# Two orders of VectorE passes, and a spread of reciprocals by float32r products, in a two-layer transformer kernel

## The reference

```python
def reference(x, f, ...):                      # x, f: (16, 256, 256)
    # layer 0
    q = x + embed[stage][:, :, None]
    c = softmax(q @ f^T) @ f                   # first attention, one head of 256
    x = x + attn0(c)                           # 16 heads of 16, causal, rotary q and k
    #   probs = softmax(scores / 4); out = probs @ v; out @ w_out^T + b_out
    c2 = x @ W_cat[cat] + b_cat[cat]
    x = x + fp4_ffn(c2)                        # 256 -> 704 -> 256, all operands quantised:
    #   scale = max|.| over 16 / 6; q = grid(x / scale) * sign * scale
    # layer 1
    y = zX * lap_x(x) + zY * lap_y(x) + zR * x * (1 - x)   # "field", neighbours with reflection
    x = x + attn1(rmsnorm(y) * g)              # 16 heads of 64, segments of 128, 16 memory rows
    x = x + moe(experts_of(x))                 # gelu, 16 experts by index, then top 2 of 8
    return x
```

## Time and profile before

| | |
|---|---|
| median of 3 runs | 2429.3 us (2426.37 to 2429.45) |
| the profiled execution, its own time | 2426.79 us |
| its span | 2424.7 us |
| busy share of the span: PE, PEld, DVE, ACT, POOL | 93%, 84%, 76%, 53%, 42% |
| chain that ended last, by engine | PE 58%, DVE 19%, POOL 8%, issue 7%, ACT 6%, DMA 1% |
| mean granted TensorE clock | 0.975 |
| layer 0 in the trace | up to about 790 us; one batch every 41.8 us |
| layer 1's attention | about 700 to 1500 us; one batch every 44.9 us |
| experts | from about 1500 us on |

### The profile page before, as it was taken

One profiled execution on the slowest core, in us unless ns is written; L12 is line 12 of the kernel. 1 busy time (PEld: TensorE's weight loads), 2 busy tenths in 40 slices (PEclk: granted clock), 3 DMA queues, 4 the chain that ended last, 5 costly groups with the idle time before them and its releaser, 6 DMA issues.

```text
span 2424.7 us, 53715 instructions
## 1 busy us (share of the span) xinstructions
PE 2248.6 (93%) x18240; PEld 2041.3 (84%) x18240; DVE 1852.2 (76%) x5119; ACT 1292.3 (53%) x3839; POOL 1019.9 (42%) x1078
## 2 busy tenths in 40 slices
PE   3799999999976899999999999899999999999999
PEld 2688878888865778888888887899999999999999
DVE  5878888888878666666666765578878888888876
ACT  1667666666662455655555554433336555555522
POOL 5535454454525455455555553033332222222073
PEclk8999999999997899999999999999999999999999
DMA  4523333333330322222222222222126777777443
GB/s 138 182 85 107 103 95 116 91 113 95 99 110 3 99 57 58 72 60 58 70 64 57 66 57 75 64 36 43 39 94 213 233 235 237 233 232 239 142 120 124
DMA packets 203301, 267.36 MB, mean 110 GB/s; under 512 B 61670, under 2 KB 171510, under 8 KB 192278
## 3 DMA queue, kind: packets, MB, share of 16 engines
q1 hardware_dynamic: 194166, 245.27, 33.4%
q0 software_dynamic: 8864, 18.66, 2.9%
HBM read 175.84 MB, written 43.94 MB: 91 GB/s over the span
## 4 chain that ended last, share of the span: by engine, by line
PE 58%; DVE 19%; POOL 8%; issue 7%; ACT 6%; DMA 1%; SPq 0%; POOLq 0%; DVEq 0%; ACTq 0%
PE bank L55 48%; PE bank L136 6%; POOL P L1796 2%; DVE xe L928 2%; PE bank L1322 2%; DVE Ph L821 2%; DVE tb L1654 1%; DVE qm L917 1%; DVE xe L933 1%; DVE sgs L955 1%; ACT P L1495 1%; PE bank L1362 1%; ACT Ph L657 1%; DVE rot0s L881 1%; DVE hb L965 1%
## 5 line engine op out<-in xcount | busy, mean ns | idle before, releaser
L1495 ACT ACTIVATE P<-P,mx 128x144 f32<-128x144 f32 x512 | 206.2, 405 | 229.2 <-DVE mx L1616 228.2
L2642 POOL DMA_INDIRECT xE<-d_y,ixs x78 | 112.1, 1437 | 336.2 <-PE bank L136 300.7
L55 PE MATMUL bank<-xD_hi,w1e_lo 128*128 128x256 f32 x880 | 251.1, 285 | 0.0
L55 PE MATMUL bank<-w2e_hi,hrD_hi 128*128 128x256 f32 x880 | 249.0, 283 | 0.0
L55 PE MATMUL bank<-w2e_lo,hrD_hi 128*128 128x256 f32 x880 | 248.9, 283 | 0.0
L55 PE MATMUL bank<-w2e_hi,hrD_lo 128*128 128x256 f32 x880 | 248.9, 283 | 0.0
L55 PE MATMUL bank<-xD_lo,w1e_hi 128*128 128x256 f32 x880 | 245.9, 279 | 0.0
L55 PE MATMUL bank<-xD_hi,w1e_hi 128*128 128x256 f32 x880 | 245.6, 279 | 0.0
L1127 POOL TENSOR_TENSOR xe<-xe 128x704 f32<-128x704 f32 (+3 forms) x64 | 88.0, 1375 | 353.9 <-DVE xe L936 353.7
L1796 POOL TENSOR_TENSOR P<-P,rs 128x512 f32<-128x512 f32 x128 | 133.1, 1040 | 246.0 <-DVE rs L1625 243.5
L2251 ACT ACTIVATE hD<-bank,b1E 128x256 f32<-128x256 f32 x312 | 127.0, 473 | 197.2 <-PE bank L55 182.8
(11 more groups left out here) (324 smaller groups left out, 7959.7 us busy)
## 6 DMA issues: line engine op xcount, KB each, us to landing
w1raw<-in_ew SPq DMA_DIRECT2D x39, 1024.0 KB, 5.9
w2raw<-in_ew SPq DMA_DIRECT2D x39, 1024.0 KB, 4.9
stack<-d_rot SPq DMA_DIRECT2D x256, 96.0 KB, 2.7
K<-Kn SPq DMA_DIRECT2D x256, 72.0 KB, 2.0
d_rot<-QKh SPq DMA_DIRECT2D x64, 256.0 KB, 3.1
Q<-Qn SPq DMA_DIRECT2D x256, 64.0 KB, 2.0
d_ys<-oE SPq DMA_DIRECT2D x39, 256.0 KB, 2.6
d_rot<-QKl SPq DMA_DIRECT2D x32, 256.0 KB, 3.1
```

The source lines that it names most:

```text
L55: inst = e.matmul(out, l, r, start=k == 0, stop=k == len(pairs) - 1)
L1495: inst = e.activation(P1[t % 2][:, n, :], P1[t % 2][:, n, :], ACT.Exp, bias=mx1[t % 2][:, 2 * g + sg:2 * g + sg + 1], scale=-1.0, accum_ou ...
L2642: e.indirect_dma_start(out=xE[q % 2][c], out_offset=None, in_=d_y, in_offset=bass.IndirectOffsetOnAxis(ap=ixs[r % 4][:, c:c + 1].bitcast(U ...
```

## The change

It has three parts. In layer 0, `invert_sums` makes the reciprocal, its high part rounded to float32r and the rest, side by side in a zeroed buffer `rsp` of 128 columns a half; it stands behind the first half's scales in slot 7. PE turns the 128 columns, ACT copies 128 rows as float32r, and `spread_sums` multiplies by `sel0r`, which has two ones a row of output (for the high and the low part), in float32r. In layer 0's order, the second half's scales move from slot 0 to the end of slot 7, ahead of the first half's last two steps; PE takes `values` and `turn_sums` ahead of `first_values`, and ACT `sums_copy` ahead of `x1_high`. In layer 1, `rotate(b + 1, 2)` and `rotate(b + 1, 3)` come earlier and the field's three passes later.

```diff
-        w_out0, rsT, OT0 = tile("w_out0", 2, 256), tile("rsT", 256), tile("OT0", 2, 256)
+        w_out0, rsT, OT0 = tile("w_out0", 2, 256), tile("rsT", 256, dt=F32R), tile("OT0", 2, 256)
-        tile("space_q", 552)
+        rsp, sel0r = tile("rsp", 2, 128, dt=F32R), tile("sel0r", 2, 128, dt=F32R)
+        tile("space_q", 40)
@@ turn_sums, spread_sums (PE)
-                turn(e, [(banks[6][0:16, st * 128:st * 128 + 128], rs0[b % 2][:, st, :]) for st in range(2)]
+                turn(e, [(banks[6][:, st * 128:st * 128 + 128], rsp[:, st, :].bitcast(F32)) for st in range(2)]
-                    inst = e.matmul(halves(7)[:, G, :], sel0[0:16, G, :], rsT[0:16, :], start=True, stop=True)
+                    inst = e.matmul(halves(7)[:, G, :], sel0r[:, G, :], rsT, start=True, stop=True)
@@ layer 0's loop (PE)
-                    if p == 0:
-                        first_values(b + 1)
-                        turn_sums(b - 1)
                     if p % 2 == 0:
                         values(P // 2 - 1)
+                    if p == 0:
+                        turn_sums(b - 1)
+                        first_values(b + 1)
@@ ACT
-                e.activation(rsT[0:16, :], banks[6][0:16, 0:256], ACT.Copy).then_inc(c_rsT, 1)
+                e.activation(rsT, banks[6][:, 0:256], ACT.Copy).then_inc(c_rsT, 1)
+                e.activation(sel0r, sel0, ACT.Copy)
                         first_copy(b + 1)
+                        sums_copy(b - 1)
                         x1_high(b + 1)
-                        sums_copy(b - 1)
@@ invert_sums (DVE)
                 e.wait_ge(c_P, 16 * (b + 1))
-                e.reciprocal(rs0[b % 2], rs0[b % 2]).then_inc(v_ri, 1)
+                if b:
+                    e.wait_ge(p_rsT, b)
+                else:
+                    e.wait_ge(g_V, 2)
+                inv, hi, lo = rs0[b % 2], rsp[:, :, 0:16], rsp[:, :, 16:32]
+                e.reciprocal(inv, inv).then_inc(*vs.up())
+                e.wait_ge(s_v, vs.n)
+                e.tensor_copy(hi, inv).then_inc(*vs.up())
+                e.wait_ge(s_v, vs.n)
+                e.tensor_tensor(lo, inv, hi.bitcast(F32), ALU.subtract).then_inc(v_ri, 1)
@@ layer 0's loop (DVE)
                     if p == 0:
-                        hidden_scales(b - 2, 1)
                         x1_low(b + 1)
                         hidden_steps(b - 2, 1)
                     if p == 7:
                         hidden_scales(b - 1, 0)
+                        invert_sums(b)
                         gated(b - 1, 1, 0)
                         gated(b - 1, 1, 1)
                         multiply(b - 1, 1, 0)
                         hidden_steps(b - 1, 0, (0,))
                         multiply(b - 1, 1, 1)
+                        hidden_scales(b - 1, 1)
                         hidden_steps(b - 1, 0, (1, 2))
-                        invert_sums(b)
@@ layer 1's loop (DVE), ahead of the maxima
                     if s == 2:
-                        rotate(b + 1, 2)
+                        rotate(b + 1, 3)
@@ behind the maxima
                     if s == 2:
-                        rotate(b + 1, 3)
+                        field(entering(b))
+                        field_sum(entering(b))
                     copy_turned(t)
+                    if s == 1:
+                        rotate(b + 1, 2)
-                    if s == 1:
-                        field(entering(b))
-                        field_sum(entering(b))
```

More of the change, by code:

```diff
@@ L313, in sync_ab @@
             load_in(0)
-            for dst, src in ((raw0, "w_qkv0"), (b_qk0, "b_qk0"), (rot0, "rot0k"), (sel0[0:16], "sel0"),
+            for dst, src in ((raw0, "w_qkv0"), (b_qk0, "b_qk0"), (rot0, "rot0k"), (sel0, "sel0"),
                              (w_out0, "w_out0"), (b_out0, "b_out0")):
@@ L1147, in pool_ab @@
             e.wait_ge(s_const, 1)
+            e.memset(rsp.bitcast(F32), 0.0)
             for i in range(2):
@@ L2744 @@
     A["w_out0"] = T2(np.ascontiguousarray(g["L0_attn_w_out"].T[rows]))
-    sel = np.zeros((16, 2, 128), np.float32)
+    sel = np.zeros((128, 2, 128), np.float32)
     for r in range(256):
-        sel[rows[r] // 16, r // 128, r % 128] = 1.0
+        sel[rows[r] // 16::16, r // 128, r % 128][0:2] = 1.0
     A["sel0"] = sel
```

## The result

The changed kernel takes 2437.29 us (median of 12 runs, 2432.41 to 2440.34). The kernel before took 2429.64 us (median of 12, 2425.57 to 2430.81) on the same chip. The ratio is 1.0033, with a 95% interval of 1.0025 to 1.0040, so the change makes the kernel slower by 7.7 us. The profiled execution took 2439.2 us, with a span of 2437.1 us, where before's had 2424.7. The spans differ by 12.4 us. 4.7 us of that is where each profiled execution happens to lie in its own runs.

The account below looks back on a forecast made before the run. VectorE was taken to set the time for 12 us of each layer 0 round, so PE savings there gain nothing. Terms 17.6 - 15.0 + 1.7 + 0.4 = +4.7 us gave 2434.0 us on the median, range 2412 to 2446.

Parts of the forecast that it names:

- The mechanism: Layer 0 loses as VectorE's steps take turns with POOL's delayed passes; layer 1 gains from an earlier rotation; chance 0.45.
- Layer 0's border: Layer 0, slot 7 to slot 1's maxima: those maxima come 1.26 us later a round, +17.6 us over 14 borders.
- rival B: Layer 0: holds don't add up, so it gains 0 to 0.5 us a round; 2413 us in all; chance 0.20.
- D: Layer 0: step 0 misses POOL's first pass or POOL keeps the port; +1.66 to +2.1 a round, 2440 to 2446; chance 0.18.
- E: PE's bound is elsewhere and both layers' new orders are absorbed; 2430 us; chance 0.05.
- list of signs: Expected changed profile, including steps 1 and 2 at 1.5 and 1.6 us, layer 0 rounds of 43.0, layer 1 of 43.7.
- I count them at nothing: Layer 0, PE: shorter spread (0.55 to 0.8 us) and removed PT wait (0.34 us) gain nothing, hidden behind VectorE.
- Layer 1: Earlier rotation 2 ends PE's wait for it; gain 1.15 us a round (0.9 to 1.35), -15.0 us over 13 rounds.
- Rival C: Layer 1 gives nothing, the field holding slot 2's copy by what the rotation frees; +19.7, 2449 us; chance 0.12.
- The join: Where the layers join: two more layer 0 borders cost +2.5, moving the field returns 0.8; +1.7, bounds -3 and +5.
- The start: Kernel start: one more ACT copy of 256 columns and one memset ahead of the first weights; +0.4 us.

Follow-up runs that it names:

- filled wait: Changed kernel plus three PE products per round, result overwritten, ahead of the wait for `hq` in slot 1; ratio 0.9980 to the kernel before.
- (a): Kernel before with layer 1's new order, and layer 0's three second-half steps moved behind the next slot's maxima; ratio 0.9910 to the kernel before.
- (b): Changed kernel with the second scales back in slot 0 and the second-half steps moved behind the next maxima; ratio 0.9929 to the kernel before.
- (c): Changed kernel, scales left in slot 7, with the second-half steps moved behind the next maxima; ratio 0.9953 to the kernel before.
- second set: The next four follow-up kernels after the first four, each run in turn with the kernel before on one chip; before's median there 2429.4 us.

## Why the prediction was right, and where it was not

The forecast was 2434.0 us with 2412 to 2446, "slower" the likeliest at 0.51. Measured were 2437.3 us and a ratio of 1.0033. The mechanism holds. The sum was +4.7 us. Measured were +7.7 on the medians and +12.4 between the traces. That the medians came so near is in part luck, as the sum at the end of this section shows.

**Layer 0's border** came out as it was laid down. The table shifts the changed trace by 29.87 us, so that the first scales' small pass stands where it stood before, 427.31:

| | forecast | measured |
|---|---|---|
| gate starts | 428.62 | 428.54 |
| step 2 of the first half ends | 433.87 | 433.87 |
| POOL starts | 434.10 | 434.01 |
| step 0 asked for | 435.53 | 435.50 |
| POOL's second pass ends | 438.05 | 438.02 |
| POOL's third pass ends | 439.69 | 439.66 |
| step 2 ends | 440.07 | 440.04 |
| slot 1's maxima start | 439.99 | 439.97 |

A round at full clock takes 42.98 us, where 43.0 was said. (Step 1 took the 1.91 us of the sum, 436.52 to 438.43, not the 1.5 us of the prediction's list of signs.) So rival B (no turns), D (step 0 misses the first pass) and E (neither part does anything) are out. The kernel with only the scales moved shows that this one call makes nearly all of it, 1.09 of 1.2 us. The one with POOL's passes cut shows that they are what it runs into.

**The step that failed** is "I count them at nothing", on PE's savings. It is right that they gain no time: with the scales back, PE's 1.3 us turned wholly into waiting, and the round was 0.27 us longer, not shorter. It is wrong that they are harmless. The wait for `hq` was forecast (1 to 2 us), but its price was put at zero because the scores behind it wait anyway. Its real price is the clock: behind 1.7 and 0.6 us of idle PE, close together, the clock falls in one round of two, and such a round takes 1.0 us more. Per round of layer 0 that is 1.2 + 0.5 = 1.7 us, and 22.0 us in thirteen, where the sum had 16.4 for as many. The filled wait takes the 0.5 away, as far as the traces go, and nothing else. With the scales moved but none of PE's savings, the clock never fell, so the savings have a part in it. In this trace before, the clock of layer 0's even rounds was 1.00, so no row of that stretch showed the price; no step of the prediction asked what idle PE costs.

**Layer 1**: -15.0 forecast, -15.9 measured over twelve rounds (1.33 us each, for 1.15). This is nearly the upper bound of 1.35. The late copy in slot 2 does make PE wait, 0.26 us where I took off 0.2, but a wait of 0.17 us for ACT in the slot behind it is gone. All in all PE's waits in these twelve rounds went from 23.0 us to 8.3. The field's three passes end 3.26 us after they start (3.2 forecast). Rival C is out.

**The join**: +1.7 forecast with -3 to +5, for its two borders. The stretch that I can measure, from batch 14's slot 4 on, holds the fourteenth ordinary border as well, so the forecast for it is +3.0, with -1.7 to +6.3. Measured were +6.0, near the top. The busy time of this stretch (before, and changed):

```profile
656.07:887.54 231.47, 180.48 (x1296) 153.42 (x1296) 168.81 (x460) 108.63 (x341) 104.23 (x105) 0.87 0.26 73
```

```profile
680.50:917.95 237.45, 180.81 (x1292) 155.20 (x1292) 171.01 (x464) 109.05 (x341) 105.28 (x104) 0.85 0.25 71
```

PE is busy as long as before, so the 6 us are waits. Long waits for `hq` and a low clock are there in both: up to 5.5 us and 0.87 before, up to 7.1 us and 0.85 now.

The same stretch took: before 231.5 us, moved scales alone 237.2, layer 1's order alone 237.1, that and the early reciprocal 236.0, layer 0's part alone 236.8, the scales back 236.2, the split and spread alone 233.0, the whole change 237.4, the filled wait 237.5, POOL's passes cut 229.3; with the steps late, 231.8 (a), 234.1 (b) and 234.6 (c). So moved scales and layer 1's order each cost over 5 us there, and do not add up. Which wait takes which part is not settled: each is a single trace, and the border's price times two, as I took it, is not how the join works.

**The start**: +0.4 forecast, +2.4 measured at the maxima of slot 4 in batch 1. Seven traces have the changed kernel's code up to there, and lie 0.2 to 3.9 us later than before. Three others have the old code up to there, and lie 1.1 to 1.7 us later as well. So what the start costs is known to a microsecond or two at best, and no run was made for it.

**The sum again**, in us:

| stretch | before | changed | difference | forecast |
|---|---|---|---|---|
| start, to slot 4 of batch 1 | 111.5 | 113.9 | +2.4 | +0.4 |
| layer 0, thirteen rounds | 544.5 | 566.6 | +22.0 | +16.4 |
| join | 231.5 | 237.4 | +6.0 | +3.0 |
| layer 1, twelve rounds | 539.1 | 523.1 | -15.9 | -15.0 |
| the rest, mostly the experts | 998.1 | 996.0 | -2.1 | 0 |

On the medians 4.7 of the 12.4 go, because before's profiled execution lay below its median and the changed kernel's above. So the median came within 3.3 us of the forecast, with the term of layer 0 off by 5.6; the experts' 2.1, which the change did not touch, and the place of the profiled executions helped.

## What to carry to other kernels

- Before moving VectorE work from one side of a POOL hand-over to the other, lay both engines' passes side by side in time. A single small pass asked for inside a POOL pass can cost what is left of that pass (1.56 us for a 0.18 us copy), and a row of passes can cost a POOL pass for each. Not every pass is held: beside POOL's passes the reduction for the second scales took 0.88 us (at 433.11 in the trace before), as it does with POOL idle (426.40), and the maxima, which read a PSUM bank, weren't held either. Those held here read SBUF alone (copy, steps, the scales' small pass). The work moved out of such a place (1.3 us of hold) is worth nothing if it delays POOL's start into the passes that follow.
- PE time saved ahead of a wait for another engine is no gain, and may be a loss: two stretches of idle PE close together can lower its clock for the work behind them. Read the granted clock by round, and where two rounds of the same work differ, look at PE's wait ahead of the slow products.
- A change of several parts should be run in parts: here layer 1's part alone is 0.9948 and the rest 1.0122. Layer 1's order with the steps behind the next maxima is the fastest kernel found, at 0.9910.

## What was not expected of the hardware

- PE's clock fell to its lower level behind waits of 1.72 and 0.62 us (0.9 us of work between them), in six rounds of twelve with the same code and the same waits. It never fell with 0.43 and 0.62 us (PE filled), nor with waits of 0.8 and 0.6 us that lie 6.5 us apart (scales moved alone), nor with 1.61 and 0.40 us that lie 3.0 us apart (scales back in slot 0). It fell in two of twelve with 1.59 and 0.41 us that lie 1.2 us apart (late steps, c). In the changed kernel two low rounds and two full ones follow each other in turn.
- The same program took 2429.4 us on the chip of the second set, 2444.5 and 2440.3 on those of the other two. The traces put the difference in the experts: from the end of layer 1 to the end of the program 880 to 888 us in the traces of the second set and the first two kernels, 899 to 906 in the others, with the rounds of both layers equal to 0.05 us. In one such stretch of 901 us PE's clock was 0.98 and it was busy 876 us, where it had been 0.99 and 868 in 884. Why is not known; no run here was made for it.
